# Layers 2a and 4 of a graph-network kernel: a chunk picked by one-hot matmuls in every second super-chunk

## The chip, the cores and the metric

The program runs on one NeuronCore of one Trainium2 chip. The metric is the device time of one execution in microseconds, the median of the runs shown. TensorE, VectorE, ScalarE and GpSimd are called PE, DVE, ACT and POOL in the profile; SyncE is SP, and ACTq and SPq are the rows in which ACT and SP issue transfers.

## The reference

12500 nodes with 64 features, 200000 edges sorted by destination. Four residual layers of a graph network, each followed by a layer norm. What matters here is that every layer sums messages of edges into their destination nodes:

```python
aggr = jax.ops.segment_sum(x[src], dst, num_segments=N_NODES)          # layer 0 (pass 0)
messages = _mlp(concat([nodes[row], nodes[col], edge_features]), ...)   # layer 1 (pass 1)
agg = jax.ops.segment_sum(h[src], dst, num_segments=N)                  # layer 2, twice (passes 2 and 3)
for r in range(16): msg += h_src * (etypes == r)[:, None] @ weight[r]   # layer 3 (pass 4)
```

Pass 2 sums the 64-wide rows x[src]; pass 4 sums rows of (x @ weight[r])[src] with r the type of the edge.

## The kernel before, in words

**Tiling.** The edges lie in 1568 chunks of 128. Eight chunks are a super-chunk (super, `SUPER`), of which there are 196. The kernel makes five passes over all supers (`p` = 0 to 4); layer 2 takes two of them, 2 and 3 ("2a" is pass 2). Within a pass the 12500 nodes are handled in 50 units of 250, each in four stages spread over four supers by `SCHEDULE` (L65): unit u begins at super 4u + 5, later 4u + 3, 4u + 1, and the last two at 4u. Stage 0 lies on the first of these four supers.

**One super.** POOL (`gathers`, L573) issues one indirect DMA per chunk: 128 rows of the pass's table by their source index, into one of four slots of G. Slot s % 4 is free when super s - 4 has been summed (semaphore `summed`). Some supers get their last chunk another way: SP and ACT copy its 128 rows one by one (`some_rows`, L519 and L777), SP in the supers of `SP_SUPERS`, ACT in those of `ACT_SUPERS`; in passes 2 and 4 ACT issues 16 such copies at the end of its work on every super. TensorE (`sum_window`, L1480) multiplies the eight chunks with one-hot matrices of their destinations into one bank PAG; VectorE (`add_straight`) adds PAG to the sums AGG and writes the one-hots of the next super.

**The chunk that is not gathered.** In passes 2 and 4 the chunk DENSE_CHUNK (the seventh) of some supers is picked out of X, which holds all node rows on the chip as 100 blocks of 125 nodes x 64. For the i-th such chunk, begun at super s (`dense_begin`, L115):

- ACT loads the chunk's 128 numbers, copied to 125 partitions (`dense_rows_in`, L795), two uses ahead.
- DVE writes 13 one-hot matrices into HOTS, the upper halves of the slots of G (`dense_one_hot`, L1308, four instructions). There is one HOTS.
- PE multiplies them with 8 blocks of X each: 13 parts of 512 columns (the last of 256), all into one bank DACC (`dense_parts`, L1561). The profile shows two matmul instructions a part.
- DVE masks the block that is meant and reduces DACC to 128 x 64 (`dense_pick`, L1296). In pass 2 this is the chunk.
- In pass 4 PE turns it (DTURN), ACT copies the turned rows to XT, PE multiplies with all 16 relation matrices (DMAPS, two matmuls), and DVE masks the type and reduces (`dense_message`, L1322).

Before, a chunk begins every five supers and takes five supers for its parts (`DENSE_PIECES`: 3, 3, 2, 3, 2); its use is 6 (pass 2) or 8 (pass 4) supers after its begin.

**What sets the order.** Every engine runs one program, in order, `straight()`, written super by super:

- PE (L1728): the node work of `SCHEDULE[s]`, the sum of super s (which waits for DVE's add of super s - 1, for the gathers and for row copies), then `dense_stage` (L1573): the turn, the map matmuls, the parts.
- DVE (L1348): the add of super s - 1, the one-hots of super s + 1, the node work, then `dense_stage` (L1333): pick, message, one-hots of the next chunk.
- ACT (L815): the node work, then `dense_stage` (L802): the load of the next numbers, the copy of a turned chunk; then `some_rows`. In pass 2, stage 3 of a unit on ACT copies PE's result to HT (L721), and DVE's statistics of the unit (L1196) wait for it; stage 2 goes PE products, ACT scaling, DVE norm, ACT root.
- The part k = 0 waits on PE for the one-hots (`dense_hot`) and for the pick of the chunk before (`dense_row`); the pick waits for the last part (`dense_summed`).

The tables that the picking needs (DV16, BLOCK8, TYPE) are made in pass 0 by `dense_tables` (L1276), and DV16 goes through DRAM (`dense_tab`).

Of the kernel before, what the change touches and what calls it, by code (L numbers as in the profile page):

```python
# [33 lines left out]
D = 64  # L34
H = 128
# [21 lines left out]
DENSE_READY = 77  # L57
# [51 lines left out]
DENSE_PIECES = [range(-(-DENSE_PARTS * k // DENSE_STEP), -(-DENSE_PARTS * (k + 1) // DENSE_STEP)) for k in range(DENSE_STEP)]  # L109
DENSE_LEAD = {2: DENSE_STEP + 1, 4: DENSE_STEP + 3}  # L110
# [4 lines left out]
def dense_begin(p, s):  # L115

    if p in DENSE_LEAD and s + DENSE_LEAD[p] in DENSE_USES:
        return DENSE_USES.index(s + DENSE_LEAD[p])
    return None


def gnn_kernel(nc, x, xT, src_c, src_e, dst_c, dst_r, type_c, type_e, src_d, efT, W1, b1, W2, b2, mW1, mb1, mW2T, mb2,
               uW1, ub1, uW2, ub2, Wl1, Wr1, sb1, gamma, beta, Wl2, Wr2, sb2, Wrel, out):
    ctx = ExitStack()
    with ctx:
# [59 lines left out]
        o += 2 * (SUPERS + P)  # L185

# [9 lines left out]
        o += P // 2  # L196
        CF = HT[:, o:o + DENSE]
# [4 lines left out]
        o += DENSE  # L202
        assert o <= N
# [77 lines left out]
        def pb(name, shape):  # L281
# [80 lines left out]
        dense_out = sem("dense_out")  # L362
# [8 lines left out]
            (DSRC, src_d), (IDX3[:, :], type_c), (SRC_E[:, :], src_e), (IDX3_E[:, :], type_e),  # L371
# [64 lines left out]
        def dense_count(p, i):  # L436

            return DENSE_LAYERS.index(p) * DENSE + i

# [38 lines left out]
        def _(sp):  # L478
# [59 lines left out]
            with sp.If(regular > 0):  # L538
# [5 lines left out]
                sp.wait_ge(far_stored, all_stored(0))  # L544
                piece = P // (SP_SUPERS[1][1] - SP_SUPERS[1][0])
# [26 lines left out]
        def _(pool):  # L572
# [46 lines left out]
        def _(act):  # L619
# [175 lines left out]
            def dense_rows_in(p, i):  # L795
# [19 lines left out]
            def straight():  # L815
                registers = [act.alloc_register(f"act_row{k}") for k in range(ACT_AT_ONCE)]
                starts = []
                for p in range(LAYERS):
# [5 lines left out]
                    if p in DENSE_LAYERS:  # L824
                        act.wait_ge(dense_out, 16)
# [73 lines left out]
        def _(dve):  # L899
# [376 lines left out]
            def dense_tables():  # L1276

                c0, step_ = DENSE_USES[0] * GROUP + DENSE_CHUNK, DENSE_STEP * GROUP
                columns = slice(c0, c0 + step_ * (DENSE - 1) + 1, step_)
# [5 lines left out]
                link(nc.vector.tensor_scalar(CF, SRC[:, columns], -(HALF - 1) / 2, 1.0 / HALF, ALU.add, ALU.mult))  # L1285
# [3 lines left out]
                link(nc.vector.scalar_tensor_tensor(TYPE[:, :], SRC[:, columns], -float(R), IDX3[:, columns],  # L1289
                                                    ALU.mult, ALU.add))  # L1290
                link(nc.vector.tensor_scalar(PART_P, IOTA[0:HALF, 0:DENSE_PARTS], float(P), None, ALU.mult))
                assert step[0] == DENSE_READY

            masked = [0]

            def dense_pick(p, i):  # L1296
# [4 lines left out]
                                               .to_broadcast([P, DENSE_BLOCKS, D]), BLOCK8[:, i:i + 1], halves(DACC),  # L1301
# [3 lines left out]
                nc.vector.tensor_reduce(DROWS[n % 2], DACC.rearrange("p (j c) -> p c j", c=D), AX.X, ALU.add)\  # L1305
# [526 lines left out]
```

## Time and profile before

| | |
|---|---|
| median of 3 runs | 9513.84 us (9511.21 to 9514.28) |
| profiled execution, its own time | 9512.51 us |
| its span, first to last instruction | 9510.6 us |
| mean granted TensorE clock | 0.68 of 2.4 GHz |
| passes 2 and 4, first to last gather | 3859.7 to 5695.6 us, 7665.0 to 9498.9 us |

The profile is one execution, taken by the hardware profiler. Times are in us unless marked ns. Idle time stands behind a bar or in square brackets, with what ended it; "issue" means that the engine waited for nothing that the profile shows. The program lines are those of the kernel; every matmul is recorded at L1445 and every gather at L585, so they are told apart by their tiles.

### The profile page before, as it was taken

Reading aid. Unit: us, or ns where it says so; the run is one execution under the profiler, and the core shown is the slowest. Engines: PE = TensorE matmul, PEld = TensorE weight load, DVE = VectorE, ACT = ScalarE, POOL = GpSimd, SP = SyncE. Lnnn points to the kernel's source line nnn. Section 1 sums busy time; section 2 is a strip of 40 time slices with the busy share of each in tenths; the row PEclk is TensorE's granted clock in tenths of the full one; section 3 lists DMA queues with packets and bytes.
Section 4 is the critical chain, followed back from the end, with each engine's and each line's share of the span. In section 5 each row is a group of like instructions: output and inputs, shape, how many; then the busy total and the mean of one; then the engine's idle time right before and its main releaser. Section 6 shows DMA issues by size and latency. Waiting matters only on the chain.

```text
span 9510.6 us, 132941 instructions
## 1 busy us (share of the span) xinstructions
PE 5855.1 (62%) x25994; PEld 4473.6 (47%) x25995; DVE 2980.1 (31%) x6598; ACT 1307.9 (14%) x2823; POOL 7095.0 (75%) x7518
## 2 busy tenths in 40 slices
PE   4555455566666666566666665666666656666665
PEld 3444444456666666443444444555455533333333
DVE  2222222234444444222222223333333322222332
ACT  1111111111111111000000002222222200000000
POOL 7777777767777777777777777777777757777777
PEclk6555655577777777788788875555555568777777
DMA  3111111133333333111111112222322211111111
GB/s 77 34 34 34 36 34 35 34 88 94 96 94 95 96 95 95 39 32 33 32 33 32 33 31 71 81 80 81 85 80 81 84 33 31 31 31 31 30 31 29
DMA packets 468282, 529.44 MB, mean 56 GB/s; under 512 B 229285, under 2 KB 296361, under 8 KB 467377
## 3 DMA queue, kind: packets, MB, share of 16 engines
q0 software_dynamic: 240448, 346.67, 16.2%
q1 hardware_dynamic: 93825, 88.20, 3.3%
q10 hardware_dynamic: 133167, 85.97, 3.1%
q14 instruction: 634, 5.19, 0.2%
q8 instruction: 208, 3.41, 0.1%
HBM read 442.89 MB, written 77.30 MB: 55 GB/s over the span
## 4 chain that ended last, share of the span: by engine, by line
POOL 70%; issue 23%; PE 3%; ACTq 2%; ACT 1%; DVE 1%; DMA 1%; SPq 0%; POOLq 0%; DVEq 0%
POOL G L585 70%; PE PH L1445 1%; PE PAG L1445 1%; ACTq L443 1%; ACTq L451 1%; SPq L486 0%; PE NA L1445 0%; ACT G L845 0%; PE NB L1445 0%; DVE G L1244 0%; DMA G<-h_tab,SRC 0%; ACT STG L746 0%; DMA rel_tab<-STG 0%; ACT XT L656 0%; ACT Y L729 0%
## 5 line engine op out<-in xcount | busy, mean ns | idle before, releaser
L1445 PE MATMUL PAG<-OH,G 128*64 128x96 f32 (+2 forms) x12050 | 2095.3, 359 | 2726.0 <-DMA G<-in_x,SRC 758.8
L1445 PEld LDWEIGHTS PAG<-OH,G 128*64 128x64 f32 (+2 forms) x12050 | 1907.9, 235 | 3037.9 <-issue 2503.3
L585 POOL DMA_INDIRECT G<-far_tab,SRC x1527 | 1440.9, 944 | 485.3 <-issue 465.5
L585 POOL DMA_INDIRECT G<-in_x,SRC x1525 | 1441.1, 945 | 476.5 <-issue 464.6
L585 POOL DMA_INDIRECT G<-h_tab,SRC x1524 | 1438.9, 944 | 479.4 <-issue 462.9
L585 POOL DMA_INDIRECT G<-rel_tab,IDX x1469 | 1386.0, 943 | 499.1 <-issue 448.0
L585 POOL DMA_INDIRECT G<-x_tab,SRC x1469 | 1387.9, 945 | 463.5 <-issue 447.6
L1032 DVE TENSOR_TENSOR AGG<-AGG,PAG 64x96 f32 (+2 forms) x980 | 245.3, 250 | 4708.6 <-PE PAG L1445 4692.6
L1445 PE MATMUL PH<-X,G 125*128 125x512 f32 (+1 forms) x1976 | 1134.7, 715 | 13.5 <-DVE G L1315 13.4
L1445 PE MATMUL PAG<-OH,HT 128*128 128x96 f32 x3126 | 619.3, 380 | 573.8 <-ACT HT L838 573.8
L996 DVE TENSOR_TENSOR OH<-CONST,DREL 128x768 f32<-128x768 f32 x980 | 926.6, 946 | 3.0 <-issue 2.2
L1445 PEld LDWEIGHTS PAG<-OH,HT 128*128 128x128 f32 x3126 | 576.3, 284 | 620.8 <-ACT HT L838 620.2
L1445 PEld LDWEIGHTS PH<-X,G 125*128 125x128 f32 x1976 | 436.8, 241 | 516.7 <-issue 488.0
L1445 PE MATMUL PH<-HT 128*128 128x128 f32 x3136 | 568.1, 357 | 51.4 <-DVE HT L1070 51.2
L1445 PEld LDWEIGHTS PH<-HT 128*128 128x128 f32 x3136 | 549.7, 272 | 58.4 <-DVE HT L1070 57.9
L1445 PE MATMUL PH<-wrel,XT 64*125 64x512 f32 (+1 forms) x552 | 445.7, 971 | 147.3 <-ACT XT L656 147.3
L1377 DVE TENSOR_TENSOR HT<-PH,G 128x1024 f32<-128x1024 f32 (+1 forms) x196 | 234.1, 1195 | 599.9 <-DMA G<-far_tab,SRC 591.2
L838 ACT ACTIVATE HT<-HT 128x1024 f32<-128x1024 f32 x196 | 206.5, 1054 | 1546.5 <-DVE HT L1377 1546.5
L1445 PEld LDWEIGHTS PH<-wrel,XT 64*125 64x125 f32 (+1 forms) x552 | 151.8, 292 | 350.1 <-issue 180.1
L845 ACT ACTIVATE G<-G 128x1024 f32<-128x1024 f32 (+1 forms) x196 | 201.7, 1029 | 828.9 <-DVE G L1244 484.3
L1070 DVE SCALAR_TENSOR_TENSOR HT<-HT,FIRST,CONST 96x1024 f32<-96x1024 int16 x196 | 248.5, 1268 | 37.2 <-DMA HT<-near_tab 37.2
L1244 DVE TENSOR_TENSOR G<-G,CONST 128x1024 f32<-128x1024 f32 (+1 forms) x196 | 232.4, 1186 | 85.7 <-DMA G<-h_tab,SRC 85.3
(194 smaller groups left out, 4414.3 us busy)
## 6 DMA issues: line engine op xcount, KB each, us to landing
GROWS<-x_tab SPq DMA_DIRECT2D x4096, 0.2 KB
GROWS<-rel_tab SPq DMA_DIRECT2D x4096, 0.2 KB
GROWS<-in_x SPq DMA_DIRECT2D x3584, 0.2 KB
GROWS<-h_tab SPq DMA_DIRECT2D x3456, 0.5 KB
rel_tab<-STG ACTq DMA_DIRECT2D x200, 250.0 KB
GROWS<-far_tab SPq DMA_DIRECT2D x3072, 0.5 KB
GROWS<-x_tab ACTq DMA_DIRECT2D x3072, 0.2 KB
GROWS<-rel_tab ACTq DMA_DIRECT2D x3072, 0.2 KB
```

The lines of the kernel that those rows point to most:

```text
L443: eng.reg_load(registers, starts[r:r + 1, e:e + len(registers)])
L451: eng.dma_start(GROWS[e:e + 1, b, 0:w].bitcast(U8), table[bass.ds(start, 4 * w)].unsqueeze(0))\
L585: pool.indirect_dma_start(out=slot_of(p, h)[:, j, 0:tabs[p].shape[1]], out_offset=None, in_=tabs[p], in_offset=bass.IndirectOffsetOnAxis(a ...
L838: nc.scalar.activation(mix, mix, ACT.Relu).then_inc(relu_done, 1)
L845: nc.scalar.activation(G[:, h, 0:chunks, :], G[:, h, 0:chunks, :], ACT.Relu)\
L996: return nc.vector.tensor_tensor(OH[:, b, :, :], IOTA_P.unsqueeze(1).to_broadcast([P, GROUP, WIN]), d.unsqueeze(2).to_broadcast([P, GROUP, ...
L1032: return nc.vector.tensor_tensor(dst, dst, PAG[0:m, 0:WIN], ALU.add)
L1070: nc.vector.scalar_tensor_tensor(MIXT[0:WIN, b, :], DROW[:, b, :], FIRST[0:WIN, bass.ds(t, 1)], PIOTA_P[0:WIN, :].to_broadcast([WIN, SUPER ...
L1244: nc.vector.tensor_tensor(rows_, rows_, CROW_P.unsqueeze(1).to_broadcast([P, chunks, H]), ALU.add)\
L1377: nc.vector.tensor_tensor(HID[:, h % 2, 0:edges], PH[h % 2][:, 0:edges], G[:, h, 0:edges // P, :].rearrange("p j c -> p (j c)"), ALU.add)\
L1445: return nc.tensor.matmul(dst, lhsT, rhs, start=start, stop=stop, skip_group_check=True)
```

## The change

The chunk is picked in every second super of passes 2 and 4, not in every fifth. The parts are spread over two supers (7 and 6), the use is 3 supers after the begin in pass 2 and 5 in pass 4. The steps per pass are a table now, with code for pass 0 that is not used (it is not in `DENSE_STEP`). The source indices and types of the picked chunks are loaded in two further arrays, and the tables' scratch moves to the start of HT, so SP waits for the table's copy (`dense_in`) before pass 1 streams into that place.

```diff
-DENSE_STEP = 5
-DENSE_LAYERS = [2, 4]
-DENSE_USES = range(DENSE_STEP + 3, SUPERS - 1, DENSE_STEP)
-DENSE = len(DENSE_USES)
+DENSE_STEP = {2: 2, 4: 2}
+DENSE_LAYERS = sorted(DENSE_STEP)
+DENSE_LEAD = {p: step + (3 if p == 4 else 1) for p, step in DENSE_STEP.items()}
+DENSE_USES = {p: range(SHARED + 1 if p == 0 else DENSE_LEAD[p], SUPERS - 1, step) for p, step in DENSE_STEP.items()}
+DENSE_SUPERS = sorted(set().union(*DENSE_USES.values()))
+DENSE = len(DENSE_SUPERS)
...
-DENSE_LEAD = {2: DENSE_STEP + 1, 4: DENSE_STEP + 3}
...
+def dense_parts_of(p, k):
+    return range(-(-DENSE_PARTS * k // DENSE_STEP[p]), -(-DENSE_PARTS * (k + 1) // DENSE_STEP[p]))
...
         early = [
-            (DSRC, src_d), (IDX3[:, :], type_c), ...
+            (DSRC, src_d), (CSRC, src_dc), (CTYPE, type_dc), (IDX3[:, :], type_c), ...
...
                 sp.wait_ge(far_stored, all_stored(0))
+                sp.wait_ge(dense_in, DENSE_IN)
...
-                       [DENSE_USES if p in DENSE_LAYERS else () for p in range(LAYERS)])
+                       [DENSE_USES[p] if p in DENSE_LAYERS else () for p in range(LAYERS)])
...
             def dense_stage(p, s):          # DVE
-                i = dense_begin(p, s - DENSE_STEP)
+                i = dense_begin(p, s - DENSE_STEP[p])
                 if i is not None:
                     dense_pick(p, i)
-                i = dense_begin(p, s - DENSE_STEP - 2)
+                i = dense_begin(p, s - DENSE_STEP[p] - 2)
                 if p == 4 and i is not None:
                     dense_message(i)
                 i = dense_begin(p, s)
                 if i is not None:
                     dense_one_hot(p, i)
...
             def dense_stage(p, s):          # PE: the turn at s - step, the maps at s - step - 1, then
-                for k in range(DENSE_STEP):
+                for k in range(DENSE_STEP[p]):
                     i = dense_begin(p, s - k)
                     if i is not None:
-                        dense_parts(p, i, DENSE_PIECES[k])
+                        dense_parts(p, i, dense_parts_of(p, k))
```

## Rows read from the trace of the kernel before

**Rows 1.** The page: busy time by engine, and the chain that ended last.

```profile
PE 5855.1 (62%) x25994; PEld 4473.6 (47%) x25995; DVE 2980.1 (31%) x6598; ACT 1307.9 (14%) x2823; POOL 7095.0 (75%) x7518
...
POOL 70%; issue 23%; PE 3%; ACTq 2%; ACT 1%; DVE 1%; DMA 1%; SPq 0%; POOLq 0%; DVEq 0%
```

**Rows 2.** Groups of POOL: gathers of passes 2 and 4 (busy us, mean ns | idle).

```profile
L585 POOL DMA_INDIRECT G<-x_tab,SRC x1469 | 1387.9, 945 | 463.5 <-issue 447.6 <-DMA x_tab<-XS 15.5 <-PE PAG L1445 0.3
L585 POOL DMA_INDIRECT G<-rel_tab,IDX x1469 | 1386.0, 943 | 499.1 <-issue 448.0 <-DMA rel_tab<-STG 51.1
```

**Rows 3.** Stretches of passes 2 and 4: length, busy us by engine, PEclk, DMA.

```profile
3860.00:5770.00 1910.00, 1181.42 (x5196) 769.57 (x5196) 518.80 (x1095) 140.08 (x456) 1432.97 (x1517) 0.79 0.16 33
...
7660.00:9510.00 1850.00, 1139.11 (x4542) 689.94 (x4542) 537.30 (x1144) 74.32 (x238) 1385.96 (x1469) 0.78 0.16 31
```

**Rows 4.** Waits: us in total, times, longest.

```profile
PE PAG L1445 <- DMA G<-x_tab,SRC: 481.1, 110, 16.6
...
DVE BST L1196 <- ACT HT L721: 212.8, 50, 5.9
```

**Rows 5.** Timeline of pass 2, DVE: the pick's mask, the next one-hots (start, us).

```profile
4636.44 0.75 DVE L1300 SCALAR_TENSOR_TENSOR PH<-IOTA,BLOCK,PH 128x512 f32<-128x512 f32 x1 [0.28 <-PE PH L1445]
...
4637.84 2.31 DVE L1315 SCALAR_TENSOR_TENSOR G<-GROWS,PIOTA,CONST 125x512 f32<-125x512 int16 x4
```

**Rows 6.** Timeline of pass 2, PE: stage 2, a sum, three parts, stage 3.

```profile
4649.75 0.48 PE L1445 MATMUL NB<-wr,XT 64*125 64x128 f32 x2
...
4652.11 1.18 PE L1445 MATMUL PAG<-OH,G 128*64 128x96 f32 x12
...
4653.55 2.84 PE L1445 MATMUL PH<-X,G 125*128 125x512 f32 x6
4656.23 0.61 PE L1445 MATMUL NA<-IDENT,Y 125*128 125x125 f32 x4
```

**Rows 7.** Timeline of pass 4: the map matmuls, what follows them, the message.

```profile
8439.51 1.98 PE L1445 MATMUL PH<-wrel,XT 64*128 64x512 f32 x4
...
8441.42 2.84 PE L1445 MATMUL PH<-X,G 125*128 125x512 f32 x6
8441.53 1.29 DVE L1325 SCALAR_TENSOR_TENSOR PH<-IOTA,TYPE,PH 128x1024 f32<-128x1024 f32 x1 [0.70 <-PE PH L1445]
...
8442.86 1.22 DVE L1330 TENSOR_REDUCE G<-PH 128x64 f32<-128x1024 f32 x1
```

**Rows 8.** Timeline of pass 2: stage 2 products, ACT's row copies, stage 3's copy and statistics.

```profile
4611.09 0.70 PE L1445 MATMUL NA<-wl,Z 64*125 64x128 f32 x4
...
4615.69 5.34 ACTq L451 DMA_DIRECT2D GROWS<-x_tab  x16
...
4621.51 0.38 ACT L721 ACTIVATE HT<-NA 128x250 f32<-128x250 f32 x1 [6.91 <-PE NA L1445]
4622.03 0.43 DVE L1196 BATCH_NORM_STATS2 BST<-NA 128x6 f32<-128x250 f32 x1 [2.69 <-ACT HT L721]
```

**Rows 9.** Stretches: ten us of pass 2 (columns as in rows 3).

```profile
3937.00:3947.00 10.00, 6.61 (x21) 4.28 (x22) 6.71 (x15) 0.20 (x1) 7.54 (x8) 0.51 0.20 39
```

**Rows 10.** Timeline of pass 2, PE: work behind an idle stretch (in brackets).

```profile
3939.73 2.79 PE L1445 MATMUL PAG<-OH,G 128*64 128x96 f32 x16 [4.71 <-DMA G<-x_tab,SRC]
3943.18 4.97 PE L1445 MATMUL PH<-X,G 125*128 125x512 f32 x6 [0.67 <-DVE G L1315]
...
3977.14 1.77 PE L1445 MATMUL PAG<-OH,G 128*64 128x96 f32 x16 [1.75 <-DMA G<-x_tab,SRC]
3978.84 2.93 PE L1445 MATMUL PH<-X,G 125*128 125x512 f32 x4
...
4633.41 1.34 PE L1445 MATMUL PAG<-OH,G 128*64 128x96 f32 x14 [1.64 <-issue]
...
4634.85 1.56 PE L1445 MATMUL PH<-X,G 125*128 125x512 f32 x4
```

**Rows 11.** Timeline of set-up, SP: one load of a small array.

```profile
43.12 0.47 SPq L486 DMA_DIRECT2D wrel<-in_Wrel  x1
```

More of the change, by code:

```diff
@@ L202, in gnn_kernel @@
         o += DENSE
+        assert o <= 2 * SUPER
+        o = 2 * SUPER + 3 * H
+        HOTS0 = HT[0:HALF, o:o + 2 * SUPER].rearrange("p (h j c) -> p h j c", h=SLOTS, c=P)
+        o += 2 * SUPER
+        VROWS0 = [HT[0:HALF, o + k * D:o + (k + 1) * D].bitcast(I16) for k in range(V_BUFS)]
+        o += V_BUFS * D
+        DROWS0 = [HT[:, o + k * (D + 1):o + (k + 1) * (D + 1)] for k in range(2)]
+        o += SUPER - V_BUFS * D
+        X0 = HT[0:HALF, o:o + 2 * UNITS * D].rearrange("p (b c) -> p b c", c=D)
+        o += 2 * UNITS * D
         assert o <= N
@@ L436, in dense_count, with dense_column, dense_hots, dense_v @@
         def dense_count(p, i):
-            return DENSE_LAYERS.index(p) * DENSE + i
+            return sum(len(DENSE_USES[q]) for q in DENSE_LAYERS if q < p) + i
+        def dense_column(p, i):
+            return DENSE_SUPERS.index(DENSE_USES[p][i])
+        def dense_hots(p):
+            return HOTS2 if p else HOTS0
+        def dense_v(p, n):
+            return VROWS2[n % V_BUFS] if p else VROWS0[n % V_BUFS]
+        def dense_rows(p, n):
+            return DROWS2[n % 2] if p else DROWS0[n % 2][:, 0:D]
         def row_starts(eng, registers, p, r, e):
@@ L805, in dense_stage @@
                     act.wait_ge(prep, DENSE_READY)
-                    act.dma_start(dense_tab, DV16).then_inc(dense_out, 16)
+                    act.dma_start(dense_tab, DV16).then_inc(dense_in, 16)
+                if p == 0 and s == 12 and 0 in DENSE_LAYERS:
+                    act.wait_ge(dense_in, DENSE_IN)
+                    dense_rows_in(p, 0)
+                    dense_rows_in(p, 1)
                 i = dense_begin(p, s)
-                if i is not None and i + 2 < DENSE:
+                if i is not None and i + 2 < len(DENSE_USES[p]):
                     dense_rows_in(p, i + 2)
-                i = dense_begin(p, s - DENSE_STEP - 1)
+                if p == 4:
+                    i = dense_begin(p, s - DENSE_STEP[p] - 1)
                 if p == 4 and i is not None:
@@ L1550, in sum_straight @@
                 dense = None
-                if p in DENSE_LAYERS and s in DENSE_USES:
-                    i = DENSE_USES.index(s)
+                if p in DENSE_LAYERS and s in DENSE_USES[p]:
+                    i = DENSE_USES[p].index(s)
                     if p == 4:
@@ L1563, in dense_parts @@
                 n = dense_count(p, i)
+                if p == 0 and i == 0:
+                    pe.wait_ge(dense_in, DENSE_IN)
                 for k in parts:
@@ L1573, in dense_stage @@
             def dense_stage(p, s):
-                i = dense_begin(p, s - DENSE_STEP)
+                if p not in DENSE_LAYERS:
+                    return
+                i = dense_begin(p, s - DENSE_STEP[p])
                 if p == 4 and i is not None:
@@ L1732, in straight @@
                         pre_straight(0)
-                    if p in DENSE_LAYERS:
+                    if p and p in DENSE_LAYERS:
                         pe.wait_ge(x_kept[p - 1], UNITS)
```

71 lines of the change are left out of this document (39 added, 32 removed).

## The prediction

> **What bounds the kernel now.** I read the page's busy shares and its chain first: POOL is busy 75% of the span, and the chain that ended last is 70% POOL and 23% "issue" [rows 1]. So the time is the number of gathers times their step. The groups of POOL give the step: in pass 2 (gathers from x_tab, which is x2_tab in the code) 1469 gathers are busy 1387.9 us with 447.6 us of issue between them, (1387.9 + 447.6) / 1469 = 1.25 us each; pass 4 (rel_tab) is the same [rows 2]. A super-chunk (super) in these passes has 1469 / 196 = 7.49 gathers, 9.37 us; two have 18.74 us, four 37.5 us. The stretches of the two passes then show what stands beside it: TensorE busy 1181 of 1910 us and 1139 of 1850 us, VectorE 519 and 537 us, at a granted clock of 0.79 and 0.78 [rows 3]. What TensorE waits for most in pass 2 is the gather: 481.1 us in 110 waits [rows 4]. The kernel is gather-bound with TensorE idle a third of the time.
>
> **What the change removes.** Uses per pass go from 38 to 96 (supers 3, 5, ..., 193) in pass 2 and 95 (5, 7, ..., 193) in pass 4: 58 + 57 = 115 gathers, 115 x 1.25 = 144 us of POOL. POOL's need falls to (1469 - 58) / 196 x 2 x 1.25 = 18.0 us for two supers in either pass.
>
> **What it adds, as a loop.** The picked chunk has one set of one-hots, one accumulator bank and program order, so its work is a serial loop: VectorE picks chunk i out of the bank and only then writes the one-hots of chunk i + 1; TensorE waits for them, multiplies 7 parts in one super and 6 in the next, and only then may VectorE pick again. Before, the loop had five supers, 46.8 us of gathers, to go round in; now it has two. So I add it up, at full clock:
>
> - Pick and one-hots on VectorE: the mask starts at 4636.44, the one-hots at 4637.84 and last 2.31 [rows 5]: 1.40 + 2.31 = 3.7 us, with 0.1 for two hand-overs 3.8.
> - Parts: three parts are 6 matmul instructions, and the next work starts 4656.23 - 4653.55 = 2.68 us later, 0.447 each [rows 6]. Seven parts (14) are 6.2 us; six, the last of half width (worth 11), 4.9.
> - The sum of one super: 4653.55 - 4652.11 = 1.44 us [rows 6]. The even super's sum falls into VectorE's 3.8 us; the odd super's stands between the two sets of parts.
>
> Pass 4 adds, per use, the message: its mask and reduction take 8444.08 - 8441.53 = 2.55 us on VectorE, and since message i - 1 stands between pick i and one-hots i + 1 on that queue, it is in the loop. The two map matmuls (4 instructions) take 8441.42 - 8439.51 = 1.91 us on TensorE [rows 7]. The turn and ScalarE's copy of it fall into VectorE's part and the 7 parts, and cost nothing. **Loop of pass 4:** 3.8 + 2.55 + 6.2 + 1.44 + 1.91 + 4.9 = 20.8 us. That is over POOL's new 18.0 and over the old 18.74, so POOL waits for slots instead, and each of the 95 rounds costs 2.1 us more than now: +196 us.
>
> **Pass 2** has node work in the loop. Units begin on odd supers, so stages 1 and 3 fall on even supers (where a round starts) and 0 and 2 on odd ones, by turns. Round A (stages 1, 2): TensorE does the stage 2 matmuls in front of the odd sum, 4652.11 - 4649.75 = 2.36 us [rows 6]: 3.8 + 6.2 + 2.36 + 1.44 + 4.9 = 18.7. Round B (stages 3, 0): VectorE's statistics of stage 3 are queued ahead of the pick and wait for ScalarE's copy, which is queued behind 16 row transfers that ScalarE issues in 5.34 us after the stage 2 of the super before. From the end of the stage 2 products (4611.09 + 0.70) to the end of the statistics (4622.03 + 0.43) the trace has 10.7 us [rows 8]; only 1.44 + 4.9 of it is covered by the odd sum and parts, so the pick starts 4.4 us late. That ScalarE is late here already is seen in the waits: the statistics wait for this copy 212.8 us, 50 times [rows 4]; today a late gather hides it. B = 4.4 + 3.8 + 6.2 + 1.44 + 4.9 = 20.7. A + B = 39.4 against 37.5 now (36.0 by POOL): +1.9 x 48 = +91 us.
>
> **The clock.** TensorE will now stand still once a round: 1.7 us in A (flip and sum end near 2.1), some 6 us in B, and in pass 4 about 2.5 and 1.8 us with the turn between. What a stop costs the trace shows only in other places, so I bound it. Around an idle of 4.71 us the clock was 0.51 (the 1.2 GHz level) over ten us [rows 9]; the sum behind it took 2.79 us and 6 instructions 4.97 [rows 10], at full clock 1.44 and 2.84 [rows 6]: about 3.5 us lost. After an idle of 1.75 us the sum began warm, but the 4 instructions behind it took 2.93 instead of 1.56: 1.4 us lost. After an idle of 1.64 us nothing was lost (1.34 for 14, then 1.56 for 4) [rows 10]. So a short stop costs 0 to 1.4 us, a long one 1.4 to 3.5. I take 0.7 for A, 2.4 for B (the middle of the long ones) and 2.0 for pass 4, whose two stops lie between: (0.7 + 2.4) x 48 = +149, 2.0 x 95 = +190.
>
> The Trainium skill (TensorE: Matmul & The Clock Gate, "HAM oscillation") speaks against the change here: waits between groups of matmuls put the array back to its slow state, and each group then starts slow. By that rule, every round paying the long price of 3.5 us, the clock term would be 191 x 3.5 = 669 us instead of 339; the row with 1.64 us of idle disagrees for short stops [rows 10].
>
> **At nothing.** VectorE's 115 further picks and ScalarE's 115 further row broadcasts are otherwise in idle time (VectorE is under a third busy [rows 3]); without that cover a broadcast would cost about the issue of a row copy, 5.34 / 16 = 0.33 us [rows 8], 115 x 0.33 = 38 us. The SyncE queue's new wait for the table stands in front of pass 1's streams, and the table is written at super 6 of pass 0, some 1800 us earlier. The tables' move within HT and their greater width change only set-up. Two more loads are in SyncE's queue before TensorE's first work, at about 0.5 us each as the load in [rows 11] shows: +1 us. At the end of each pass the last four supers have no parts and their gathers are ahead: I take off half of a pair's 18.74 us, about -10 us each.
>
> **Sum.** 91 + 149 + 196 + 190 - 20 + 1 = +607 us. Against the profiled execution's 9512.5 us (span 9510.6; the median of the runs, 9513.8, is 1.3 above) that is 10120 us.
>
> **Rivals.**
> - *The clock stays up.* With less idle time TensorE may hold 2.4 GHz throughout: only the loops count, 91 + 196 - 19 = +268, 9780 us. For it: the row with 1.64 us of idle. Against it: B's stop is longer than the 4.71 us that cost 3.5. 20%. The Trainium skill (same page, "Part 1") says activity releases the throttle, which would lead here.
> - *Pass 2 hides its loop.* If ScalarE's rows end earlier (a late round moves them too), B is 18.4 or less and pass 2 runs near POOL's 18.0: between -19 (B 18.4) and -72 us (36.0 for four supers) there, say -40; with pass 4 at full clock or as forecast, 196 or 386, and the ends' -19: 9650 to 9840. The 10.7 us come from one place where the gather set the pace. 12%.
> - *POOL stays the bound: faster.* It needs both loops under 18.0 us per two supers; then 144 us go: 9370 us. For it: POOL is the busiest engine, and VectorE has two thirds of its time free; four slots buffer any single late round. Against it: buffers don't help a mean, and pass 4's loop is 2.8 us over with nothing but durations of [rows 5 to 7] in it. It decides in the pick: if the next one-hots did not stand behind pick and message, 6.3 us would leave the loop. 6%. The Trainium skill (Perfetto Trace Analysis, "Identifying the Most-Contended Engine") would have the engine of highest occupancy relieved first, which leads to this rival.
> - *The change does less than it says* (the other code path is taken): the trace shows gathers left out and L1315 at work, so this path runs; under 1%.
>
> **Numbers.** The forecast has 60%. Its own range: clock terms from 1.4 to 3.5 us a round (191 rounds: 267 to 669) on top of the 268 give 10050 to 10450. The range of 8 in 10 takes in the full-clock case and the upper part of the second rival: 9720 to 10450. A measurement of this kernel tells 0.2% (19 us) from no change. Faster 0.06 (the third rival), same 0.02 (pass 2's gain and pass 4's loss would have to cancel), slower 0.92.
>
> **What would show it.** Right: POOL's step stays 1.25 us busy-to-busy, but G's gathers in passes 2 and 4 wait for PE PAG (they hardly do now); those passes last 2050 and 2200 us or more, the others as before; from one pick to the next it is 20 us or more; TensorE waits for the one-hots once a round; in pass 4 mask, reduction, message and one-hots follow each other without a gap for 6.3 us. The clock term is read from the granted clock of the two passes and from the parts' duration (0.447 or 0.85 us an instruction). Wrong: gathers that never wait for PAG, or pass 4 under 1900 us.

## The result, and the profile after

| | before | after |
|---|---|---|
| median | 9514.06 us (4 runs, 9511.21 to 9514.41) | 10135.98 us (4 runs, 10131.73 to 10139.86) |
| profiled execution, its span | 9512.51, 9510.6 us | 10131.73, 10129.8 us |

The change makes the kernel 6.5% slower: ratio 1.0654, 95% interval 1.0639 to 1.067. 10120 was forecast. The profiled executions are 619.2 us apart, and the sums below are made against that. The total came out nearly right, but its terms did not all do so.

Where the time went is read from the first gather of each pass. Three of the four lines that follow are POOL's timeline of the kernel after (start, us, what the gather waited for).

```profile
3861.30 0.94 POOL L622 DMA_INDIRECT G<-x_tab,SRC  x1 [17.57 <-DMA x_tab<-XS]
5869.89 0.94 POOL L622 DMA_INDIRECT G<-h_tab,SRC  x1 [22.43 <-DMA h_tab<-STG]
7828.60 0.94 POOL L622 DMA_INDIRECT G<-rel_tab,IDX  x1 [55.15 <-DMA rel_tab<-STG]
```

The fourth is from the kernel before; with its first gathers of passes 2 and 4 (3859.7 and 7665.0) it bounds the same passes.

```profile
5710.34 0.94 POOL L585 DMA_INDIRECT G<-h_tab,SRC  x1 [14.71 <-DMA h_tab<-STG]
```

From first gather to first gather (pass 4: to the end of the span), the passes last:

| pass | before | after | difference | forecast |
|---|---|---|---|---|
| 0 and 1 | 3856.9 | 3858.5 | +1.6 | +1 |
| 2 | 1850.6 | 2008.6 | +158.0 | +230 |
| 3 | 1954.7 | 1958.7 | +4.0 | 0 |
| 4 | 1845.6 | 2301.2 | +455.6 | +376 |

The page of after: busy times, the granted clock by slices, and the chain that ended last. These answer to [rows 1].

```profile
PE 7045.0 (70%) x29326; PEld 4849.1 (48%) x29327; DVE 3515.2 (35%) x7402; ACT 1315.9 (13%) x2880; POOL 6985.0 (69%) x7403
...
PEclk6555655677777778999999955555555888888888
...
POOL 39%; PE 30%; issue 15%; DVE 9%; ACTq 4%; ACT 1%; DMA 0%; SPq 0%; DVEq 0%; POOLq 0%
```

POOL did lose work, 115 instructions and 110 us of busy time, and it is no longer what ends last: its share of the chain fell from 70% to 39%, TensorE's rose from 3% to 30%. The groups of POOL, which answer to [rows 2], say how (busy us, mean ns | idle, and what ended it):

```profile
L622 POOL DMA_INDIRECT G<-rel_tab,IDX x1412 | 1332.0, 943 | 1007.3 <-PE PAG L1490 564.8 <-issue 387.4 <-DMA rel_tab<-STG 55.1
...
L622 POOL DMA_INDIRECT G<-x_tab,SRC x1411 | 1332.3, 944 | 671.4 <-issue 405.2 <-PE PAG L1490 248.7 <-DMA x_tab<-XS 17.6
```

A gather takes what it took. New is the wait for PE PAG: 248.7 us in pass 2 and 564.8 in pass 4, where [rows 2] had 0.3 and none. POOL now waits for TensorE to free a slot. The waits over the whole span (us, times, longest), which answer to [rows 4], name the loop:

```profile
POOL G L622 <- PE PAG L1490: 825.9, 236, 9.3
DVE PH L1343 <- PE PH L1490: 708.5, 143, 5.6
...
PE PH L1490 <- DVE G L1358: 522.9, 186, 6.1
...
DVE BST L1239 <- ACT HT L758: 245.6, 49, 5.7
PE PH L1490 <- DVE G L1373: 221.0, 93, 2.7
```

VectorE's pick (L1343) waits for TensorE's last part, TensorE's first part waits for VectorE's one-hots (L1358) once in nearly each of the 191 rounds, and in pass 4 the turn waits for the message (L1373). Neither engine is full; they wait for each other in turn.

The stretches of passes 2 and 4, which answer to [rows 3] (length, busy us by engine, PEclk, DMA):

```profile
3941.00:5800.00 1859.00, 1506.11 (x6152) 832.41 (x6151) 656.61 (x1322) 124.04 (x415) 1246.21 (x1320) 0.92 0.15 30
7920.00:10080.00 2160.00, 1785.35 (x5971) 876.60 (x5970) 829.12 (x1504) 76.93 (x277) 1244.17 (x1320) 0.86 0.13 24
```

The clock is higher than before (0.79 and 0.78), with a TensorE busy for 81 and 83% of the stretch instead of 62%. It is still not full, and pass 4 has the lower one.

**One round of pass 4** in the timeline (start, us, idle before it and its releaser), which answers to [rows 5, 7]:

```profile
9021.33 0.76 DVE L1343 SCALAR_TENSOR_TENSOR PH<-IOTA,BLOCK,PH 128x512 f32<-128x512 f32 x1 [5.62 <-PE PH L1490]
...
9022.73 1.28 DVE L1368 SCALAR_TENSOR_TENSOR PH<-IOTA,TYPE,PH 128x1024 f32<-128x1024 f32 x1
9024.04 1.22 DVE L1373 TENSOR_REDUCE G<-PH 128x64 f32<-128x1024 f32 x1
9025.19 2.31 DVE L1358 SCALAR_TENSOR_TENSOR G<-GROWS,PIOTA,CONST 125x512 f32<-125x512 int16 x4
9025.42 0.40 PE L1490 MATMUL PH<-IDENT,GROWS 128*64 128x128 f32 x2 [2.66 <-DVE G L1373]
...
9027.55 9.34 PE L1490 MATMUL PH<-X,G 125*128 125x512 f32 x14 [1.73 <-DVE G L1358]
...
9036.82 1.53 PE L1490 MATMUL PAG<-OH,G 128*64 128x96 f32 x16
9038.29 1.98 PE L1490 MATMUL PH<-wrel,XT 64*128 64x512 f32 x4
...
9040.20 4.99 PE L1490 MATMUL PH<-X,G 125*128 125x512 f32 x12
...
9045.23 0.75 DVE L1343 SCALAR_TENSOR_TENSOR PH<-IOTA,BLOCK,PH 128x512 f32<-128x512 f32 x1 [5.62 <-PE PH L1490]
```

From pick to pick 9045.23 - 9021.33 = 23.9 us. Pick, message and one-hots follow each other without a gap for 6.2 us, as forecast. Then come seven parts, the sum, the maps, six parts. Only one thing departs from the loop as added up: the seven parts take 9.34 us, where 6.28 is their time at full clock (below).

The picks of pass 4 show the clock falling into this state. These are the first four and the last of 95:

```profile
7857.52 0.76 DVE L1343 SCALAR_TENSOR_TENSOR PH<-IOTA,BLOCK,PH 128x512 f32<-128x512 f32 x1 [3.71 <-PE PH L1490]
7878.20 0.76 DVE L1343 SCALAR_TENSOR_TENSOR PH<-IOTA,BLOCK,PH 128x512 f32<-128x512 f32 x1 [5.62 <-PE PH L1490]
7899.03 0.76 DVE L1343 SCALAR_TENSOR_TENSOR PH<-IOTA,BLOCK,PH 128x512 f32<-128x512 f32 x1 [5.62 <-PE PH L1490]
7922.58 0.76 DVE L1343 SCALAR_TENSOR_TENSOR PH<-IOTA,BLOCK,PH 128x512 f32<-128x512 f32 x1 [5.62 <-PE PH L1490]
...
10097.61 0.76 DVE L1343 SCALAR_TENSOR_TENSOR PH<-IOTA,BLOCK,PH 128x512 f32<-128x512 f32 x1 [5.36 <-PE PH L1490]
```

The first two rounds are 20.7 and 20.8 us, the loop at full clock to the tenth. From the third on they are 23.5 to 23.9 (the very last 25.0), and the mean of the 94 rounds is (10097.61 - 7857.52) / 94 = 23.83.

**Two rounds of pass 2**, which answer to [rows 6, 8]:

```profile
5001.58 8.47 PE L1490 MATMUL PH<-X,G 125*128 125x512 f32 x14 [6.01 <-DVE G L1358]
...
5016.47 0.76 DVE L1343 SCALAR_TENSOR_TENSOR PH<-IOTA,BLOCK,PH 128x512 f32<-128x512 f32 x1 [3.71 <-PE PH L1490]
...
5020.24 6.28 PE L1490 MATMUL PH<-X,G 125*128 125x512 f32 x14 [1.91 <-DVE G L1358]
...
5030.18 4.99 PE L1490 MATMUL PH<-X,G 125*128 125x512 f32 x12
...
5032.38 5.61 ACTq L487 DMA_DIRECT2D GROWS<-x_tab  x16
...
5035.00 0.61 PE L1490 MATMUL NA<-IDENT,Y 125*128 125x125 f32 x4
...
5038.46 0.38 ACT L758 ACTIVATE HT<-NA 128x250 f32<-128x250 f32 x1 [7.21 <-issue]
...
5038.98 0.42 DVE L1239 BATCH_NORM_STATS2 BST<-NA 128x6 f32<-128x250 f32 x1 [5.54 <-ACT HT L758]
5039.32 0.74 DVE L1343 SCALAR_TENSOR_TENSOR PH<-IOTA,BLOCK,PH 128x512 f32<-128x512 f32 x1
```

Round A (pick at 5016.47) has a stop of 1.91 us and its parts run at full clock. In round B the pick waits for the statistics, these for ScalarE's copy, and that stands behind 16 row copies: the pick starts at 5039.32, where the one of round A starts 0.11 after TensorE's next matmul, so 5039.32 - 5035.00 - 0.11 = 4.2 us late. TensorE then stands for 6.0 us, and its seven parts take 8.47 us (the line at 5001.58, one pair of rounds earlier; 8.16 in the mean of the rounds B, while A's take 6.28 every time). The mean from pick to pick is 20.62 us.

### The profile page after: what moved, and what is told of

Read it like the earlier page. It is cut to its first block, busy times and chain, and to the rows that moved or that the text cites. A ratio compares the mean times of both kernels' runs of the same rounds, so it can differ in the third digit from the quotient of the medians.

```text
span 10129.8 us, 140667 instructions
## 1 busy us (share of the span) xinstructions
PE 7045.0 (70%) x29326; PEld 4849.1 (48%) x29327; DVE 3515.2 (35%) x7402; ACT 1315.9 (13%) x2880; POOL 6985.0 (69%) x7403
## 4 chain that ended last, share of the span: by engine, by line
POOL 39%; PE 30%; issue 15%; DVE 9%; ACTq 4%; ACT 1%; DMA 0%; SPq 0%; DVEq 0%; POOLq 0%
POOL G L622 39%; PE PH L1490 25%; DVE G L1358 4%; PE PAG L1490 3%; ACTq L487 3%; DVE PH L1343 1%; ACTq L479 1%; DVE PH L1368 1%; PE NB L1490 1%; DVE GROWS L1348 1%; PE NA L1490 1%; SPq L522 0%; ACT G L888 0%; ACT Y L749 0%; DVE Y L1172 0%
## 5 line engine op out<-in xcount | busy, mean ns | idle before, releaser
L1490 PE MATMUL PH<-X,G 125*128 125x512 f32 x4966 | 2523.8, 666 | 522.9 <-DVE G L1358 522.9
L1490 PE MATMUL PAG<-OH,G 128*64 128x96 f32 (+2 forms) x11934 | 1819.4, 325 | 1423.4 <-DMA G<-in_x,SRC 765.8
L1490 PEld LDWEIGHTS PAG<-OH,G 128*64 128x64 f32 (+2 forms) x11934 | 1648.3, 210 | 1695.9 <-issue 1133.7
L622 POOL DMA_INDIRECT G<-rel_tab,IDX x1412 | 1332.0, 943 | 1007.3 <-PE PAG L1490 564.8
L1490 PEld LDWEIGHTS PH<-X,G 125*128 125x128 f32 x4966 | 1051.9, 219 | 1883.7 <-issue 1309.2
L622 POOL DMA_INDIRECT G<-x_tab,SRC x1411 | 1332.3, 944 | 671.4 <-issue 405.2
L1490 PE MATMUL PH<-wrel,XT 64*125 64x512 f32 (+1 forms) x780 | 548.1, 852 | 140.4 <-ACT XT L693 139.1
L1358 DVE SCALAR_TENSOR_TENSOR G<-GROWS,PIOTA,CONST 125x512 f32<-125x512 int16 x764 | 441.7, 640 | 17.7 <-DMA GROWS<-dense_tab 17.7
L1343 DVE SCALAR_TENSOR_TENSOR PH<-IOTA,BLOCK,PH 128x512 f32<-128x512 f32 x191 | 143.5, 751 | 708.5 <-PE PH L1490 708.5
L1490 PEld LDWEIGHTS PH<-wrel,XT 64*125 64x125 f32 (+1 forms) x780 | 187.0, 256 | 374.3 <-issue 203.0
```

The lines of the kernel that those rows point to most:

```text
L622: pool.indirect_dma_start(out=slot_of(p, h)[:, j, 0:tabs[p].shape[1]], out_offset=None, in_=tabs[p], in_offset=bass.IndirectOffsetOnAxis(a ...
L1343: nc.vector.scalar_tensor_tensor(halves(DACC), IOTA[:, 0:DENSE_BLOCKS].unsqueeze(2) .to_broadcast([P, DENSE_BLOCKS, D]), BLOCK8[:, dense_c ...
L1358: last = nc.vector.scalar_tensor_tensor(dense_hots(p)[:, h, 0:hi - lo, :], dense_v(p, n).unsqueeze(1).to_broadcast(shape), PIOTA[0:HALF, 0:1],
L1490: return nc.tensor.matmul(dst, lhsT, rhs, start=start, stop=stop, skip_group_check=True)
```

## The experiments

Each is an edit of the kernel after. Runs 1 to 7 are single executions; for 8 to 10 the median of four is given. The kernel before, run beside them, took 9512.6 to 9515.6 us. In every run the passes that its edit leaves alone came out within 9 us of those of after. The pass times and rounds named below are worked out from the traces as above.

**1. Pass 4: the message ahead of the pick.** VectorE does message i - 1 while TensorE still multiplies, so that it is no longer between pick and one-hots.

```diff
             def dense_stage(p, s):          # DVE
-                i = dense_begin(p, s - DENSE_STEP[p])
-                if i is not None:
-                    dense_pick(p, i)
                 i = dense_begin(p, s - DENSE_STEP[p] - 2)
                 if p == 4 and i is not None:
                     dense_message(i)
+                i = dense_begin(p, s - DENSE_STEP[p])
+                if i is not None:
+                    dense_pick(p, i)
```

> Pass 4 alone: VectorE computes message i - 1 before it waits for the pick, not after. Theory (pick, message, one-hots, parts, sum, maps, parts is one serial loop): the message's 2.55 us leave the loop and TensorE's stop gets as much shorter; a round of pass 4 falls from 23.9 us to 18.3 us at full clock, at most 21.3 if each round still loses 3.1 us to the clock. Kernel 9600 to 9890 us. Rival (the round is TensorE's own work at a low clock, the message is hidden): round stays 23.9, kernel 10136. Pass 2 as after the change in either case.

Measured: 9663.66 us, 472 less than after. The rounds of pass 4 fell to a median of 18.4 us (mean 18.85), pass 2 stayed. In its timeline the pick waits 2.37 instead of 5.62 us, and the seven parts run at full clock:

```profile
9007.93 0.76 DVE L1343 SCALAR_TENSOR_TENSOR PH<-IOTA,BLOCK,PH 128x512 f32<-128x512 f32 x1 [2.37 <-PE PH L1490]
...
9009.33 2.31 DVE L1358 SCALAR_TENSOR_TENSOR G<-GROWS,PIOTA,CONST 125x512 f32<-125x512 int16 x4
...
9011.70 6.28 PE L1490 MATMUL PH<-X,G 125*128 125x512 f32 x14 [1.54 <-DVE G L1358]
```

So of 5.5 us a round about half is the message (2.55) and half the clock (3.06): what took 2.55 us out of the loop also took out the stop before the turn. The mean is above the median because in 23 of the 95 rounds the seven parts still take 8 us behind the stop that is left. The order on VectorE's queue is shown to be a cause, and the serial loop with it.

**2. Pass 4: the two stops filled with idle matmuls.** Nothing leaves the loop; TensorE gets more work.

```diff
                 if p == 4 and i is not None:
+                    for _ in range(2):
+                        mm(NA[:, 0:512], IDENT[0:HALF, :], X[0:HALF, 0:DENSE_BLOCKS, 0:D])
                     pe.wait_ge(dense_row, dense_count(p, i) + 1)
                     pe.wait_ge(dense_msg, i)
                     mm(DTURN, dense_rows(p, dense_count(p, i)), IDENT[:, :]).then_inc(dense_turned, 1)
+                    for _ in range(2):
+                        mm(NA[:, 0:512], IDENT[0:HALF, :], X[0:HALF, 0:DENSE_BLOCKS, 0:D])
```

> Pass 4 alone: in each round TensorE does four further matmuls into an unused bank, two in front of the turn and two behind it, where it stood still for some 2.1 and 1.7 us. Theory (the first 8 of 14 instructions of the parts run at 1.2 GHz because TensorE stopped before): the clock stays up, the 14 take 6.2 us in place of 9.3, a round goes from 23.9 to about 21 us although 3.4 us of work were added; kernel about 9860 us. Rival (the parts start slow for another cause, such as VectorE's or the bank's traffic): round 23.9 to 24.2, kernel 10136 to 10165.

Measured: 9863.01 us, 273 less than after, with 8 more matmul instructions a round. The round of pass 4 is 20.90 us in the mean, as the loop at full clock was added up (20.8). The stretch of pass 4 has the clock at full speed, and a line of its timeline the seven parts:

```profile
7920.00:9800.00 1880.00, 1838.01 (x6684) 896.68 (x6683) 822.13 (x1494) 75.63 (x274) 1239.18 (x1314) 1.00 0.15 28
```

```profile
9021.02 6.26 PE L1490 MATMUL PH<-X,G 125*128 125x512 f32 x14
```

This is the clock's price by itself: 23.83 - 20.90 = 2.93 us a round, 278 us in the pass.

**3. Pass 2: the pick ahead of the statistics.** VectorE does `dense_stage` before the node work of the super.

```diff
                             one_hot((s + 1) % 2, DREL[:, s + 1, :]).then_inc(onehot_ready, 1)
+                        if p == 2:
+                            dense_stage(p, s)
                         for u, stage in SCHEDULE[s]:
                             node[p](u, stage)
-                        dense_stage(p, s)
+                        if p != 2:
+                            dense_stage(p, s)
```

> Pass 2 alone: VectorE does pick and one-hots of a super before the node work of that super, not after. Theory (every second round begins 4.3 us late because the pick stands behind the statistics of stage 3): the pairs of rounds fall from 41 us to 18.5 + 16.3 at full clock, under POOL's 36.0, or up to 37 with clock losses; pass 2 from 2008 us to 1780 to 1850; kernel 9905 to 9980 us. Rival (the late start is TensorE's or the gathers' and not the statistics'): pass 2 unchanged, 10136. Pass 4 unchanged.

Measured: 9938.71 us, 197 less than after. Pass 2 takes 1817.3 us, 33 less than before the change, and its rounds 18.59 us in the mean. Of the profile's waits, the one of the statistics for ScalarE's copy is gone from the long ones. The two kinds of round now have the same stop before the seven parts:

```profile
5003.51 7.97 PE L1493 MATMUL PH<-X,G 125*128 125x512 f32 x14 [1.90 <-DVE G L1358]
...
5021.67 6.28 PE L1493 MATMUL PH<-X,G 125*128 125x512 f32 x14 [1.91 <-DVE G L1358]
```

One pays 1.7 us to the clock, the other nothing. Over the pass 45 of the 96 rounds pay 1.7 us and 47 nothing; most of those that pay, but not all, have stage 3 in them.

**4. Pass 2: ScalarE's row copies in even supers only,** so that they are not in front of stage 3's copy. The other cure for the same late start.

```diff
                         dense_stage(p, s)           # ACT
-                        some_rows(p, s, registers, starts)
+                        if p != 2 or s % 2 == 0:
+                            some_rows(p, s, registers, starts)
+                        if p == 2 and s % 2 == 0:
+                            some_rows(p, s + 1, registers, starts)
```

> Pass 2 alone, VectorE's order as after the change: ScalarE issues no row copies in the odd supers and 32 in the even ones, so none stand between stage 2's root and stage 3's copy. Theory (the statistics are late because of ScalarE's 16 row copies): the late start shrinks from 4.3 us to the 1.5 us of product, copy and statistics; pairs of rounds 36.3 to 38 us, pass 2 1790 to 1880, kernel 9920 to 10010. Rival (ScalarE is late because of the products or of the store of stage 3, and the rows only stand beside it): pass 2 within 20 us of 2008, kernel 10115 to 10140.

Measured: 10070.1 us, 66 less than after: a miss in size, outside what either theory gave. The late start did shrink, to 1.5 us, and the stop of round B from 6.0 to 3.27. But in the pair shown both kinds of round now lose to the clock:

```profile
5003.37 9.17 PE L1493 MATMUL PH<-X,G 125*128 125x512 f32 x14 [3.27 <-DVE G L1361]
...
5022.73 7.97 PE L1493 MATMUL PH<-X,G 125*128 125x512 f32 x14 [1.91 <-DVE G L1361]
```

That is 2.9 + 1.7 = 4.6 us in two rounds, where the rounds of after shown above lost 2.2: the shorter stop cost more than the long one, and the stop of 1.91 us, free in after, cost 1.7. It is a dear pair. Over the pass the rounds with stage 3 lose 2.2 us in the mean (1.9 in after), and of the others 17 in 45 lose something, most of them 1.7, so that two rounds lose 2.9 us (1.9 in after). The rounds are 19.94 us in the mean. Whether the clock took all that was missing was the question of runs 5 and 6.

**5. Pass 2 as after, the stops filled.** The edit, on TensorE, ahead of part 0:

```diff
                     i = dense_begin(p, s - k)
+                    if p == 2 and k == 0 and i is not None:
+                        for _ in range(6 if any(stage == 3 for _, stage in SCHEDULE[s]) else 2):
+                            mm(PH[0][:, 0:512], IDENT[0:HALF, :], X[0:HALF, 0:DENSE_BLOCKS, 0:D])
                     if i is not None:
                         dense_parts(p, i, dense_parts_of(p, k))
```

> The change as it is, but in pass 2 TensorE fills its stop before part 0 with matmuls into an unused bank: 12 instructions (5.2 us) where stage 3 is worked on (the stop is 6.0 us there), 4 (1.7 us) in the other supers (1.9 us). Only the clock can gain by that. Theory: in the rounds with stage 3 the 14 instructions of seven parts take 6.3 us instead of 8.47, 2.2 x 48 = 106 us less, the late pick stays late by 4.2 us; pass 2 takes about 1905 us and the kernel about 10030. Rival (the long stop is the cost, not the clock behind it, or the filling costs as much as it saves): 10110 to 10150.

Measured: 10045.68 us, 90 less than after; 106 were expected. The clock of pass 2 is 1.00 in its stretch (the first line), the late pick stays (5030.09 against a matmul that starts at 5025.99), and the parts behind it take 6.28:

```profile
3941.00:5600.00 1659.00, 1637.55 (x6444) 870.57 (x6442) 612.99 (x1234) 116.08 (x388) 1164.19 (x1234) 1.00 0.16 32
...
5030.09 0.74 DVE L1343 SCALAR_TENSOR_TENSOR PH<-IOTA,BLOCK,PH 128x512 f32<-128x512 f32 x1
...
5033.84 6.28 PE L1490 MATMUL PH<-X,G 125*128 125x512 f32 x14 [0.43 <-DVE G L1358]
```

The rounds are 19.70 us in the mean, so two take 39.4: the loop of pass 2 at full clock. The clock's price in pass 2 is (20.62 - 19.70) x 2 = 1.85 us for two rounds.

**6. Run 4 with the stops filled** (6 and 4 instructions in place of 12 and 4, the rest as in runs 4 and 5 together).

> ScalarE's row copies of pass 2 only in even supers, as in the run before that gave 10070, and TensorE's stops before part 0 filled: 6 instructions (2.6 us) where stage 3 is worked on (a stop of 3.27 us), 4 (1.7 us) otherwise (1.91). Theory (that run's missing gain was taken by the clock: seven parts took 9.17 and 7.97 us instead of 6.28): 2.9 + 1.7 = 4.6 us less per two rounds brings pass 2 to the gathers' pace, about 1810 us, and the kernel to about 9935, as much as the pick ahead of the statistics gave. Rival (the 32 row copies in one super, or SyncE's, hold the pass back): 10040 to 10070.

Measured: 9942.97 us, 127 less than run 4, pass 2 1823.0 us. That is 2.65 us for two rounds, near the 2.9 that the clock took there in the mean, and not the 4.6 of the pair that the expectation went by. With the clock at 0.99 most of what run 4 missed is back. The rows of the two stops, filled:

```profile
5004.01 6.28 PE L1493 MATMUL PH<-X,G 125*128 125x512 f32 x14 [0.51 <-DVE G L1361]
...
5020.48 6.28 PE L1493 MATMUL PH<-X,G 125*128 125x512 f32 x14
```

**7. Pass 4: two buffers of one-hots.** The one-hots go to HT, which is unused in that pass, into halves used by turns, and VectorE's order is message, one-hots of the next chunk, pick. The one-hots and the parts then go by `dense_hot_at` (left out here).

```diff
+        def dense_hot_at(p, n, h):
+            if p == 4:
+                return HT[0:HALF, (n % 2) * 2 * SUPER + h * 512:(n % 2) * 2 * SUPER + (h + 1) * 512].rearrange("p (j c) -> p j c", c=P)
+            return dense_hots(p)[:, h, :, :]
...
             def dense_stage(p, s):          # DVE
+                if p == 4:
+                    i = dense_begin(p, s - DENSE_STEP[p] - 2)
+                    if i is not None:
+                        dense_message(i)
+                    i = dense_begin(p, s)
+                    if i is not None:
+                        dense_one_hot(p, i)
                 i = dense_begin(p, s - DENSE_STEP[p])
                 if i is not None:
                     dense_pick(p, i)
-                i = dense_begin(p, s - DENSE_STEP[p] - 2)
-                if p == 4 and i is not None:
-                    dense_message(i)
                 i = dense_begin(p, s)
-                if i is not None:
+                if p != 4 and i is not None:
                     dense_one_hot(p, i)
...
```

> Pass 4 alone: the one-hots get two buffers and the order on VectorE is message, one-hots, pick, so that neither the one-hots (2.31 us) nor the message (2.55 us) stand any longer between the pick and TensorE's next parts. Theory (the round of 23.9 us is the serial loop plus what the clock takes behind its stops): TensorE's own work, 1.44 + 0.5 + 6.2 + 1.44 + 1.91 + 4.9 = 16.4 us, lies under POOL's 18.0 for the gathers of two supers, the clock stays up as in the run with the message first, pass 4 takes about 1780 us and the kernel about 9615. Rival (TensorE, now waiting for gathers, stops as often and loses 3.1 us to the clock every round): 19.5 us a round, pass 4 some 1880 to 1900, the kernel 9715 to 9735. No gain over the run with the message first (9664) would say that the gathers set that run's pace already.

Measured: 9611.92 us. Pass 4 takes 1775.1 us, 70 less than before the change, and its rounds 18.05 us in the mean: that is POOL's pace (18.0). TensorE waits for gathers again, and the sum behind such a wait is slow:

```profile
9004.73 2.79 PE L1500 MATMUL PAG<-OH,G 128*64 128x96 f32 x16 [2.58 <-DMA G<-rel_tab,IDX]
```

The rival's loss is there (2.79 us; 1.53 in the round of pass 4 shown above), but now it lies in time that TensorE would have waited anyway.

**8. Runs 3 and 7 together.**

> The edit of pass 4 (two buffers of one-hots, message and one-hots ahead of the pick) together with the edit of pass 2 (the pick ahead of the statistics). If the two passes are independent, pass 2 takes 1817 us as in its own run and pass 4 about 1780: 9615 - 192 = 9424 us, about 1% faster than the kernel before. Rival (TensorE's clock takes the gain back in pass 4, as it did in the run with the rows to SyncE alone in pass 2): 9520 or more, no gain over before.

Measured: 9409.17 us against 9512.63, ratio 0.9891, interval 0.9874 to 0.9907. Both kernels are beaten. The two gains added up, 197 and 524 us off 10136, give 9415, so the passes are independent to within the 10 us by which the executions of this run differ. The profiled execution was its fastest, 9400.5 us; in it passes 2 and 4 take 1806.7 and 1774.3 us. The rival's clock did not take the gain back in pass 4. (No run here gave rows to SyncE alone; the run that lost its gain to the clock in pass 2 is run 4.)

**9. The same with 4 idle matmul instructions ahead of part 0 in pass 2.**

```diff
                     i = dense_begin(p, s - k)
+                    if p == 2 and k == 0 and i is not None:
+                        for _ in range(2):
+                            mm(PH[0][:, 0:512], IDENT[0:HALF, :], X[0:HALF, 0:DENSE_BLOCKS, 0:D])
```

> Both edits (message and one-hots ahead of the pick in pass 4, pick ahead of the statistics in pass 2) and, in pass 2, TensorE's remaining stop of 1.9 us before part 0 filled with 4 matmul instructions (1.7 us). In the run with both edits pass 2 still took 1807 us, 43 more than its 1411 gathers at 1.25 us, at a granted clock of 0.92. Theory (the clock behind that stop is what still holds TensorE above the gathers' pace): pass 2 about 1770 to 1780 us and the kernel about 9375 to 9385. Rival (the round at full clock, 18.6 and 16.4 us by turns, or late gathers set that pace): 9400 to 9415, no gain over the run with both edits.

Measured: 9373.47 us against 9515.63, ratio 0.9851, interval 0.9835 to 0.9867. Pass 2 takes 1777.9 us. The chain that ended last is that of the kernel before again [rows 1], and the groups of POOL have hardly a wait for TensorE left (pass 2, pass 4):

```profile
POOL 70%; issue 23%; PE 3%; ACTq 1%; ACT 1%; DVE 1%; SPq 0%; DMA 0%; POOLq 0%; DVEq 0%
```

```profile
L628 POOL DMA_INDIRECT G<-x_tab,SRC x1411 | 1334.6, 946 | 448.0 <-issue 430.1 <-DMA x_tab<-XS 17.7 <-PE PAG L1503 0.3
L628 POOL DMA_INDIRECT G<-rel_tab,IDX x1412 | 1332.3, 944 | 486.0 <-issue 430.9 <-DMA rel_tab<-STG 55.2
```

**10. The change with a chunk in every third super.** The gathers are 2938 in the two passes before, 2823 after and 2887 here: 64 more than after and 51 fewer than before.

```diff
-DENSE_STEP = {2: 2, 4: 2}
+DENSE_STEP = {2: 3, 4: 3}
```

> The change as it is, with one picked chunk in every third super instead of every second: 39 or so gathers more than the kernel before's... fewer picked chunks than after's and still about 51 fewer gathers than before. Theory (the loop of a picked chunk costs time only where it is longer than POOL's gathers between two picks): pass 4's loop of about 25.4 us for three supers lies under POOL's 27.6, pass 2's the same, so the kernel gains 51 x 1.25 = 64 us against before: about 9450. Rival (late picks and stops that cost clock push the rounds over POOL's pace here as well): 9514 or more.

Measured: 9455.75 us against 9512.63, ratio 0.9939, interval 0.9922 to 0.9955; 57 us gained of 64 in the gathers. The same late starts and clock losses are in it (the statistics wait 266.5 us for ScalarE's copy, the clock is 0.87 in passes 2 and 4), and the chain is POOL's all the same:

```profile
POOL 71%; issue 23%; PE 3%; ACTq 1%; DVE 1%; ACT 1%; SPq 0%; DMA 0%; POOLq 0%; DVEq 0%
```

So nothing in the picking itself is too dear. What decides is whether the loop of one picked chunk is longer than POOL's gathers between two picks.

## Why the prediction was right, point by point

The terms against what the runs showed (rounds counted as in the prediction: 48 pairs and 95 rounds; before, a pair of supers took 18.74 us):

| term | forecast | measured | from |
|---|---|---|---|
| loop of pass 2 | 91 | (39.4 - 37.48) x 48 = 92 | run 5 |
| clock in pass 2 | 149 | 1.85 x 48 = 89 | after, run 5 |
| loop of pass 4 | 196 | (20.90 - 18.74) x 95 = 205 | run 2 |
| clock in pass 4 | 190 | 2.93 x 95 = 278 | after, run 2 |
| ends of both passes | -20 | -50 | what is left of the passes' +613.6 |
| passes 0, 1 and 3 | +1 | +5.6 | first gathers |
| sum | +607 | +619 | |

- **POOL stops being the bound: right.** Its step stayed 1.25 us where it did not wait, and 813.5 us of waits for TensorE's sums stand in passes 2 and 4 where there were 0.3.
- **The loops: right, to 1 us in 92 and 9 in 205.** Both sums of durations of the trace of before came out within 0.1 us of the round at full clock (39.4 and 39.4; 20.8 and 20.90). Of the loop's parts, run 1 takes out the message alone and run 3 the late start alone, and each moves its own pass and not the other. The late start was put at 4.4 us and is 4.2.
- **The clock of pass 4: mechanism right, size wrong.** The step was "I take ... 2.0 for pass 4, whose two stops lie between"; it is 2.93, in nearly every round (3.06 in the one shown). The two stops, 2.66 and 1.73 us with the turn between, cost together nearly what a stop of 4.71 us cost in [rows 10], 3.5, rather than a mean of a short and a long one. 88 us too little.
- **The clock of pass 2: mechanism right, size wrong the other way.** The step was 0.7 for A and 2.4 for B. A lost nothing, B 2.2 in the pair shown and 1.9 in the mean; run 5 gives 1.85 for the two. 60 us too much, so pass 2 took 2008.6 us and stayed under the 2050 that were named as a sign. The row with 1.64 us of idle, which cost nothing [rows 10], was the nearer one for A.
- **The ends: 30 us more than taken off.** Outside the counted rounds pass 2 fell from 51.6 to 29.1 us and pass 4 from 65.2 to 37.3. No experiment took them apart; the figures are remainders.
- These errors, -88, +60 and +30, nearly cancel. That is luck, so a total 16 us off says less about the working than the two loops do.

The trace of before had more rows for the clock than the prediction used. One is nearer to round A than the row with 1.64 us:

```profile
3995.45 1.18 PE L1445 MATMUL PAG<-OH,G 128*64 128x96 f32 x12 [1.90 <-issue]
```

The sum behind this stop takes what it takes in [rows 6], and so do the 6 instructions after it (2.84 us, at 3996.88). Nor was 3.5 us the usual price of a long stop: from 3957 to 4010 us four stops of 3.76 to 4.56 us cost 1.6 to 2.5 us each, reckoned in the same way. And the stop of 1.75 us cost 1.6 rather than 1.4, since the sum behind it was slow too (1.77 us for 16 instructions, 1.53 at full clock).

**The rivals.** That the clock stays up at 2.4 GHz was wrong without help, and with the stops filled the loops alone cost 92 + 205 us less the ends, near the 268 that it gave. That each round pays the long price would have put the clock at 669 us; the runs give 89 + 278 = 367. The rule behind it, that a group of matmuls behind a long wait starts slow (the Trainium skill, TensorE: Matmul & The Clock Gate, "HAM oscillation"), was taken further than the page takes it, to waits of any length. It so agrees with pass 4, where the rounds lose about 3 us each (23.83 against 20.90), and not with round A, whose parts took 6.28 us behind a stop of 1.91. That pass 2 hides its loop was wrong for this order of the queues and is what run 3 made of it: 1817 us, where the rival had 1832 down to 1779 (1850.6 less 19 to 72). By the rival's own way, ScalarE's rows out of the way, it came to 1944.9 us (run 4), and to 1823.0 once the clock was kept up (run 6). That POOL stays the bound was wrong for the change, but its time, 9370 us, and the point named for it (the next one-hots behind pick and message) were right: with one-hots and message out of pass 4's loop, the statistics out of pass 2's and the clock kept up, run 9 takes 9373.47. There the rule to relieve the engine of highest occupancy (the Trainium skill, Perfetto Trace Analysis, "Identifying the Most-Contended Engine") holds; in the change as it was made it led astray, since a chain between TensorE (busy 81 and 83% in the two passes) and VectorE (35 and 38%) set the pace then, and neither share shows that. That the change does less than it says is excluded: 115 gathers are gone from the trace.

**Left open.** Why a stop of 1.9 us costs 1.7 us in one round and nothing in another (45 and 41 rounds of run 3) was not settled; the runs only show that filling it ends the loss.

## What to carry to other kernels

When work is moved from the busiest engine to two engines with idle time, add up the chain that passes between those two for one item, in program order, and compare it with the interval between items: here loops of 20.8 us (pass 4) and 39.4 us in two rounds (pass 2) against 18.0 and 36.0 made a kernel with 144 us fewer gathers 622 us slower, about 300 us by the loops themselves and 367 by the clock behind their stops, less 50 at the ends of the passes; three supers instead of two made it 57 us faster than before. If the chain is too long, look first at what stands between its links in a queue without belonging there (the message, the statistics), then at the buffer that forces the order (one set of one-hots). Last, measure the clock by filling TensorE's stops with idle matmuls: where that shortens the kernel, the price of the stops is known, and sometimes the cure.

## What the runs showed of the hardware

- **More matmuls, less time.** Eight further instructions in each round of pass 4 made the kernel 273 us shorter (run 2), 4 and 12 by turns in pass 2 90 us (run 5), and 6 and 4 on top of run 4 127 us (run 6). The granted clock went from 0.86 to 1.00 in pass 4 and from 0.92 to 1.00 in pass 2.
- **The clock's price does not grow with the stop.** In the rounds shown the seven parts took 8.47 us behind 6.01 us of idle (2.2 lost) and 9.17 behind 3.27 us (2.9 lost); over the pass such rounds lost 1.9 us in after and 2.2 in run 4. Stops of the same 1.9 us in the same kernel cost 1.7 us in 45 rounds and nothing in 41 (run 3). What a stop costs is read from the round in which it stands, not from its length.
- **It locks in.** Pass 4 began with two rounds at full clock (20.7 and 20.8), and from the third on it stayed at 23.5 or more for the rest of the pass. Runs 3 to 6, which leave pass 4 alone, fall the same way after their first one or two rounds.
- **A loss can be covered.** In run 7 a sum behind a wait for a gather still took 2.79 us instead of 1.53, and pass 4 kept POOL's pace.
